# Sparse experts planned twice: 32 tiles of the first ten sequences while the last four are routed, then 40

## The chip, the cores and the metric

One core of one Trainium2 chip runs the whole program. The metric is the device time of one execution in microseconds (us); lower is better. TensorE is called PE in the profile, VectorE DVE, ScalarE ACT, GpSimd POOL and SyncE SP.

## The reference

Two layers over x of 16 sequences x 512 tokens x 128. The first layer (a linear state recurrence and a one-of-eight linear expert) and the second layer's linear attention are the same in both kernels. What the change touches is the second layer's mixture of experts:

```python
def _moe(t, gate_w, gate_b, mlp1_w, mlp1_b, mlp2_w, mlp2_b):   # t: 8192 x 128
    logits = t @ gate_w + gate_b                               # 8 experts
    top_v, top_i = jax.lax.top_k(logits, K)                    # K = 2
    probs = jax.nn.softmax(top_v, axis=-1)
    w = zeros.at[arange(T)[:, None], top_i].set(probs)
    def body(acc, ew):
        h = _swiglu(t @ w1 + b1)     # 128 -> 512 -> 256, min(glu, 7), clip(lin, -7, 7)
        y = h @ w2 + b2              # 256 -> 128
        return (acc + we[:, None] * y, None)
...
ms = jnp.mean(x * x, axis=-1, keepdims=True)
t = (x * jax.lax.rsqrt(ms + EPS) * norm_scale)
return x + y
```

## The kernel before

The program has phases one behind the other; the last one holds the second layer. All engines have their own in-order program in it (`@block.tensor`, `@block.vector` and so on), written out by hand, and they wait for one another through counting semaphores: `need(engine, name, count)`.

*Attention and routing.* A pass n of each engine's loop works on several sequences at once, at different stages: a sequence w is projected in pass w, weighted in w + 1 and routed up to pass w + 8. Routing one sequence of 512 tokens (four slices of 128) is a chain across engines: moments (DVE), 1/sqrt by Ln and Exp (ACT), `normed` (ACT, L1661), `modulated` (DVE), `squares` and a second 1/sqrt (ACT), `payload` (ACT, L1545), `turn_pay` (PE, L2298) and `turned_pay` (ACT), `logits` (PE, L2364), `logits_kept` (ACT), `logits_back` (PE, L2376), `largest` and `chosen` (DVE), `ranks` (PE), `placed` (DVE, position `posu`), and at last eight `send`s: POOL scatters 128 payload rows each by indirect DMA into `rows_of` in DRAM (L1479), where every expert has a region of its own. The POOL's other work in this part is `products` (L1470).

*The plan.* After the last sequence PE adds up how many rows each expert has (L2404), DVE turns this into 72 tiles of 256 rows (L2024 to L2060: the expert and first row of each tile, `meta` and `packs`), SP and ACT write padding rows behind each region, and SP waits for all scatters.

*The tile loop.* 72 tiles v run through the engines. SP loads the 256 rows (`xt`, L1432). PE transposes them (`turn`, L2417), ACT copies the result to SBUF (`turned`, L1725) and copies the expert's first weights and biases out of all experts' into one of two buffers (`own_weights`, L1732). PE makes four matmuls of 128x256 (L2432). DVE adds the bias and clips, glu (L2104) and lin (L2109), ACT takes the gelu of glu (L1747), DVE multiplies (`product`, L2095). Two tiles behind, PE makes the second product (L2446, L2451), ACT scales it by the token's weight (`yw`, L1756; eight buffers), and POOL places both halves, 128 rows each, by indirect DMA into `parts` (L1504). Every fourth tile DVE computes weights and destination rows of four tiles (`weights_and_places`, L2075 to L2088).

*The tail.* When all rows are placed, SP loads `parts` sequence by sequence (L1445), DVE adds the pairs, gates them and adds them to x, and ACT's queue writes the output.

## Time and profile before

| | us |
|---|---|
| median of 3 runs | 1067.23 |
| lowest, highest | 1066.64, 1077.73 |
| span of the profiled execution, first to last instruction | 1003.5 |
| PE busy in the span | 837.3 (83%) |
| DVE busy | 827.6 (82%) |
| ACT busy | 619.4 (62%) |
| POOL busy | 563.5 (56%) |
| DMA traffic | 84.47 MB, mean 84 GB/s |

The profile is of one execution, and its own time is known by its span alone: the first row is time measured from outside, which holds what lies around the span as well. Busy shares are means over phases with different limits; rows from single stretches say more. Idle time of an engine is put down to what ended it; "issue" means that the engine waited for nothing that the profile shows. The clock column is PE's granted clock as a share of 2.4 GHz, 0.50 is 1.2 GHz.

### The profile page before, as it was taken

The page shows a single profiled execution, that of the slowest core. Times are in us where ns is not written, and L with a number is a line of the kernel's source. Part 1 is how long each engine was busy: PE and PEld are TensorE (multiplying, and loading weights), DVE is VectorE, ACT ScalarE, POOL GpSimd, SP SyncE. Part 2 cuts the span into 40 slices and gives each one's busy share as a digit, 9 for nine tenths or more (in the row PEclk, how much of TensorE's full clock was granted, in tenths as well). Part 3 has the DMA queues.
Part 4 walks back from the last instruction along what each step waited for, and adds up shares of the span by engine and source line. Part 5 has one row for each costly group of instructions (what it writes and reads, how often), then busy time and mean ns, then how long its engine had stood idle before and what let it go on. Part 6 is the DMA issues. An engine that isn't in the chain of part 4 may idle for free.

```text
span 1003.5 us, 22806 instructions
## 1 busy us (share of the span) xinstructions
PE 837.3 (83%) x7439; PEld 645.8 (64%) x7439; DVE 827.6 (82%) x2204; ACT 619.4 (62%) x1669; POOL 563.5 (56%) x573
## 2 busy tenths in 40 slices
PE   6887972899999579999999999994149999999900
PEld 6854652444454268888888888883038888889800
DVE  3987769899997586789999999997638888888848
ACT  3475128899983474587787767746236666666600
POOL 1221018568760534336888888887727676767720
PEclk9999895799999879999999999996569999999955
DMA  5230541333233050000111111111243333233168
GB/s 153 82 90 1 143 134 46 130 105 138 90 127 127 9 145 19 2 10 26 37 44 34 37 36 45 36 37 47 95 122 94 89 90 89 89 95 97 54 227 296
DMA packets 74479, 84.47 MB, mean 84 GB/s; under 512 B 14254, under 2 KB 64361, under 8 KB 72188
## 3 DMA queue, kind: packets, MB, share of 16 engines
q1 hardware_dynamic: 56492, 60.06, 19.7%
q0 software_dynamic: 8704, 18.11, 5.4%
q10 hardware_dynamic: 9168, 4.87, 1.6%
q8 instruction: 61, 1.00, 0.4%
q14 instruction: 54, 0.44, 0.2%
HBM read 59.33 MB, written 23.67 MB: 83 GB/s over the span
## 4 chain that ended last, share of the span: by engine, by line
PE 51%; DVE 6%; DMA 2%; issue 2%; POOL 1%; SPq 1%; ACT 1%; POOLq 0%; DVEq 0%; ACTq 0%
PE ps L2432 13%; PE ps L2194 11%; PE ps L2451 6%; PE ps L2210 3%; PE ps L2272 2%; PE ps L2185 2%; PE ps L2417 2%; PE ps L2331 2%; PE ps L2311 2%; PE ps L2205 1%; POOL rows_of L1479 1%; PE ps L2156 1%; PE ps L2171 1%; PE ps L2259 1%; DVE x_tok L2128 1%
## 5 line engine op out<-in xcount | busy, mean ns | idle before, releaser
L1470 POOL TENSOR_TENSOR kvb<-qk,v 128x1024 f32<-128x1024 f32 x64 | 126.7, 1984 | 74.7 <-DVE qk L1854 50.4
L1479 POOL DMA_INDIRECT rows_of<-payb,posu x128 | 144.1, 1126 | 40.6 <-issue 27.0
L1115 PE MATMUL ps<-masked,ew 128*128 128x512 f32 x256 | 129.9, 623 | 4.2 <-DVE masked L1043 3.5
L2194 PE MATMUL ps<-con,kvb 128*128 128x128 f32 x1024 | 126.0, 276 | 0.0
L2194 PEld LDWEIGHTS ps<-con,kvb 128*128 128x128 f32 x1024 | 119.4, 192 | 1.0 <-issue 1.0
L1504 POOL DMA_INDIRECT parts<-h,dest x72 | 72.8, 1011 | 55.0 <-ACT h L1756 33.3
L1043 DVE TENSOR_TENSOR masked<-f_t,wide 128x512 f32<-128x512 f32 x128 | 88.6, 710 | 9.7 <-PE ps L1115 9.4
L1830 DVE TENSOR_TENSOR qc<-ps,qk 128x1024 f32<-128x1024 f32 x64 | 78.0, 1219 | 17.9 <-PE ps L2194 17.3
L1747 ACT ACTIVATE nrm<-qk 128x512 f32<-128x512 f32 x72 | 45.4, 630 | 72.8 <-DVE qk L2104 72.7
L1504 POOL DMA_INDIRECT parts<-gx,dest x72 | 74.9, 1040 | 25.6 <-issue 23.3
L2451 PE MATMUL ps<-w,f_t 128*128 x576 | 76.1, 275 | 0.0
L2451 PEld LDWEIGHTS ps<-w,f_t 128*128 128x128 f32 x576 | 70.0, 192 | 8.3
L1115 PEld LDWEIGHTS ps<-masked,ew 128*128 128x128 f32 x256 | 43.3, 194 | 47.2 <-issue 23.9
L2432 PE MATMUL ps<-qd,ex 128*128 128x256 f32 x288 | 69.3, 384 | 0.7 <-issue 0.7
L2432 PE MATMUL ps<-qd,lg 128*128 128x256 f32 x288 | 68.3, 380 | 0.3 <-issue 0.3
L2432 PEld LDWEIGHTS ps<-qd,ex 128*128 128x128 f32 x288 | 52.8, 193 | 6.8 <-ACT qd L1725 0.9
L2432 PEld LDWEIGHTS ps<-qd,lg 128*128 128x128 f32 x288 | 51.9, 190 | 6.2 <-issue 0.5
L891 ACT ACTIVATE junk<-x_tok,stat 128x128 f32<-128x128 f32 x128 | 49.4, 387 | 10.4 <-DVE stat L1019 9.8
L2095 DVE SCALAR_TENSOR_TENSOR f_t<-qk,nrm 128x512 f32<-128x512 f32 x72 | 50.5, 701 | 6.4
L2104 DVE TENSOR_SCALAR qk<-ps,ex 128x256 f32<-128x256 f32 x72 | 31.5, 478 | 29.3 <-PE ps L2432 29.3
L2417 PE MATMUL ps<-con,kvb 128*128 128x128 f32 x144 | 28.1, 277 | 25.1 <-DMA kvb<-rows_of 25.1
L2104 DVE TENSOR_SCALAR qk<-ps,lg 128x256 f32<-128x256 f32 x72 | 31.5, 478 | 8.1 <-PE ps L2432 8.0
(354 smaller groups left out, 2237.7 us busy)
## 6 DMA issues: line engine op xcount, KB each, us to landing
wide<-hot_dram SPq DMA_DIRECT2D x16, 1024.0 KB, 4.6
kvb<-rows_of SPq DMA_DIRECT2D x72, 132.0 KB, 2.1
toep<-taps_dram SPq DMA_DIRECT2D x16, 512.0 KB, 6.1
x_tok<-in_x_dram SPq DMA_DIRECT2D x16, 256.0 KB, 3.1
out_dram<-x_tok ACTq DMA_DIRECT2D x16, 256.0 KB, 5.6
rows<-rows_dram SPq DMA_DIRECT2D x16, 192.0 KB, 3.2
kvb<-parts SPq DMA_DIRECT2D x6, 512.0 KB, 6.9
rows<-rows_dram SPq DMA_DIRECT2D x16, 128.0 KB, 4.5
```

The lines of the kernel that those rows point to most:

```text
L891: last = nc.scalar.activation(junk[j][:, c, :], source(t), ACT.Square, bias=total[:, t:t + 1], scale=float(D), accum_out=out_sq[:, t:t + 1])
L1043: nc.vector.tensor_tensor(masked[e % 4][:, :], f_t[w % W][:, :], wide[w % W][:, e, :], ALU.mult).then_inc(s["masked"], 1)
L1115: nc.tensor.matmul(ps[:, w % 2, :], ew0[:, e, :], masked[e % 4][:, :], start=False, stop=(e == E - 1)).then_inc(s["product"], 1)
L1470: nc.gpsimd.tensor_tensor(kv[g % KB][:, :, :].rearrange("p e (h d) -> p e h d", h=H), k_in, v_in, ALU.mult).then_inc(s["kv"], 1)
L1479: nc.gpsimd.indirect_dma_start(rows_of, bass.IndirectOffsetOnAxis(ap=posu[w % 2][:, slot, t:t + 1], axis=0), pay[w % PB][:, t, :], None).t ...
L1504: nc.gpsimd.indirect_dma_start(parts, bass.IndirectOffsetOnAxis(ap=dest[:, u, c:c + 1], axis=0), yw[u][:, c, :], None).then_inc(s_out[u], 16)
L1830: nc.vector.tensor_tensor(qc[g % 2][:, :, :], cum(g), q_in, ALU.mult).then_inc(s["qc"], 1)
L2095: nc.vector.scalar_tensor_tensor(act_t[v % 2][:, :, :], lin[v % 2][:, :, :], -6.0, gs[v % 2][:, :, :], ALU.max, ALU.mult).then_inc(m["a"], 1)
L2104: last = nc.vector.tensor_scalar(glu[v % 2][:, f, :], ps[:, bank, f * SP:(f + 1) * SP], w1c[v % 2][:, I2 + f:I2 + f + 1], 7.0, ALU.add, AL ...
L2194: last = nc.tensor.matmul(cum(g)[:, e, :], kv[g % KB][:, e, :], k("upto"), start=True, stop=True)
L2432: last = nc.tensor.matmul(ps[:, bank + f // 2, (f % 2) * SP:(f % 2 + 1) * SP], w1c[v % 2][:, f * P:(f + 1) * P], x_t[v % 2][:, :], start=T ...
L2451: last = nc.tensor.matmul(to, act_t[v % 2][:, j, c * P:(c + 1) * P], w2[:, bass.ds(e * (2 * D) + j * D, D)], start=False, stop=(c == S - 1 ...
```

## The change

The plan is made twice. The first one counts the rows of the first ten sequences (AW = 10), which is enough for 32 full tiles (FT = 32); it stands in DVE's last pass (n = 16) of the attention loop. The tile loop begins right behind the attention. The first 20 tiles form four rounds of five, and the routing of the last four sequences is spread over them: each engine has a `drain(v)` that does one step of the chain after a given tile. The second plan, of 40 tiles for the rest, stands behind tiles 18 to 20 on DVE; SP writes the padding before tile 28 and waits for all scatters before tile 32.

To make room the rest is rearranged. The first weights of a tile come by DMA from DRAM, 256 KB, into four buffers (WC = 4), so ACT's `own_weights` and the scaling of all weights go, and the norm scale is applied in `turned`. glu is made by ACT in two Relu of 128x256 out of PSUM instead of by DVE. The transposed rows and the result have one PSUM bank each instead of two. Results have 16 SBUF buffers (YW = 16). In the tile loop the 1/sqrt of the last sequences are powers on POOL and the two-way softmax is a tanh, all in one ACT table with the gelu.

```diff
+        room = xg[:, :, :].rearrange("p d t -> p (d t)")
         V = 8
         GT = 4
+        AW = 10
+        FT = 32
+        YW = 16
+        assert 2 * C * P * AW - E * (SP - 1) > (FT - 1) * SP
         BT = -(-(2 * TILES // S + E - 1) // V) * V
         NP = BT // V
         parts = nc.dram_tensor("parts", [(2 * TILES + S * BT) * P, D], F32).ap()
...
+            def h_of(w):
+                return h4[w % 2] if w < B - 2 else late_h[w % 2]
...
-            w1c = [q[:, :, :].rearrange("p j t -> p (j t)")[:, 0:WB] for q in (ex, lg)]
+            WC = 4
+            w1c = [(ex, lg)[j // 2][:, j % 2, :] for j in range(WC)]
-            yw = [(h4 + gx)[v // 2][:, S * (v % 2):S * (v % 2 + 1), :] for v in range(V)]
+            yw = [room[:, XT + v * S * D:XT + (v + 1) * S * D].rearrange("p (c d) -> p c d", c=S) for v in range(YW)]
...
+
+                    def pads():
+                        sp.wait_ge(s["place"], 2)
+                        sp.wait_ge(s["padrow"], 2)
+                        for e in range(E):
+                            row = sp.value_load(counts[0:1, e:e + 1], min_val=e * CAP, max_val=(e + 1) * CAP - SP)
+                            sp.dma_start(rows_of[bass.ds(row, SP), :].rearrange("(p c) d -> p c d", c=S), far[:, :, :]).then_inc(s["pads"], 16)
+
+                    def second_part():
+                        sp.wait_ge(s["pads"], 16 * E)
+                        for j in range(PB):
+                            sp.wait_ge(s_scat[j], 16 * SCATTERS * (B // PB))
+                        sp.wait_ge(s["place"], 3)
+                        need(sp, "pay_ps", B)
+
+                    for v in range(BT):
+                        if v == FT - PADS:
+                            pads()
+                        if v == FT:
+                            second_part()
+                        if v % V == 0:
+                            packed = pack_of(sp, v)
+                        at = sp.value_load(meta[0:1, v:v + 1], min_val=0, max_val=E * CAP - SP)
+                        done(sp, "x_ps", v - V)
+                        grouped(sp, "dest", v - V)
+                        sp.dma_start(xt[:, v % V, :, :], rows_of[bass.ds(at, SP), :].rearrange("(p c) d -> p c d", c=S)).then_inc(s_in[v % V], 16)
+                        e = expert_of(sp, packed, v)
+                        done(sp, "h_ps", v - WC)
+                        sp.dma_start(w1c[v % WC], a["w1"][:, bass.ds(e, 1), :].rearrange("p e i -> p (e i)")).then_inc(s_w1[v % WC], 16)
+                        if v == FT:
...
+                    for j in range(WC):
+                        sp.wait_ge(s_w1[j], 16 * (BT // WC))
+                    for v in range(BT - YW, BT):
+                        rows_out(sp, v)
...
+                    def place_rows(v):
+                        done(pool, "yw", v)
+                        for c in range(S):
+                            nc.gpsimd.indirect_dma_start(parts, bass.IndirectOffsetOnAxis(ap=dest[:, v % YW, c:c + 1], axis=0),
+                                                         yw[v % YW][:, c, :], None).then_inc(s_out[v % YW], 16)
+
+                    placed_rows = 0
+                    for v in range(ROUNDS * ROUND):
+                        r, at = divmod(v, ROUND)
+                        if at == 0:
+                            variance_root(B - 2 + r)
+                        if at == 1:
+                            square_root(B - 3 + r)
+                        if at == 4:
+                            for i in range(SCATTERS if r == ROUNDS - 1 else SCATTERS // 2):
+                                send(B - 4 + r, i)
+                        if at == 0 and r:
+                            for i in range(SCATTERS // 2, SCATTERS):
+                                send(B - 5 + r, i)
+                        if v >= 3 and v % 2:
+                            place_rows(placed_rows)
+                            placed_rows += 1
+                    for v in range(placed_rows, BT):
+                        place_rows(v)
...
+                    nc.scalar.preload_act_table_set("gelu_apprx_sigmoid_and_others")
+                    projected(B - 1)
...
-                    def own_weights(t, packed, v):
-                        if t.exists(v):
-                            e = t.expert(packed, v % V)
-                            t.done("h_ps", v - 2)
-                            t.done("lin", v - 2)
-                            nc.scalar.activation(w1c[v % 2][:, :], w1b1[:, bass.ds(e * WB, WB)], ACT.Copy).then_inc(m["w1c"], 1)
...
+                    def drain(v):
+                        r, at = divmod(v, ROUND)
+                        if r >= ROUNDS:
+                            return
+                        if at == 0:
+                            logits_kept(B - 4 + r)
+                            squares(B - 3 + r)
+                        if at == 2:
+                            normed(B - 2 + r)
+                            weigh_late(B - 4 + r)
+                            payload(B - 3 + r)
+                        if at == 3:
+                            turned_pay(B - 3 + r)
+
+                    def turned(v):
+                        if v < BT:
+                            done(act, "h_ps", v - 2)
+                            done(act, "x_ps", v)
+                            nc.scalar.activation(x_t[v % 2][:, :], ps[:, X_PS, 0:SP], ACT.Copy, scale=ns[:, :]).then_inc(m["x_t"], 1)
...
+                        turned(v + 1)
+                        if v < BT:
+                            e = expert_of(act, packed, v)
+                            bank = H_PS + 2 * (v % 2)
+                            done(act, "hg_ps", v)
+                            if v < 2:
+                                need(act, "red", B * C)
+                            for f in range(2):
+                                last = nc.scalar.activation(glu[v % 2][:, f, :], ps[:, bank, f * SP:(f + 1) * SP], ACT.Relu,
+                                                            bias=b1[:, bass.ds(e * NF + f, 1)], scale=-1.0)
+                            last.then_inc(m["glu"], 1)
+                            done(act, "a", v - 2)
+                            done(act, "glu", v)
+                            nc.scalar.activation(gs[v % 2][:, :, :], glu[v % 2][:, :, :], ACT.Gelu_apprx_sigmoid, bias=limit[:, :], scale=-1.0).then_inc(m["gs"], 1)
+                        drain(v)
+                        if v % V == V - 2 and v + 2 < BT:
+                            act.wait_ge(s["place"], 3 if v + 2 >= FT else 1)
+                            ahead = pack_of(act, v + 2)
+                        if v >= 2:
+                            u = (v - 2) % YW
+                            grouped(act, "dest", v - 2)
+                            rows_out(act, v - 2 - YW)
+                            done(act, "y_ps", v - 2)
+                            for c in range(S):
+                                last = nc.scalar.activation(yw[u][:, c, :], ps[:, Y_PS, c * D:(c + 1) * D], ACT.Copy, scale=own[:, 2, u, c:c + 1])
+                            last.then_inc(m["yw"], 1)
...
                         weighted(n - 1, 2)
+                        if n == B:
+                            rows_of_tiles(False)
                         states(n)
...
+                    done_early()
+
+                    def drain(v):
+                        r, at = divmod(v, ROUND)
+                        if v == 0:
+                            residual(B - 1)
+                        if v == 1:
+                            moments(B - 1)
+                        if r < ROUNDS and at == 1:
+                            shifted(B - 2 + r)
+                            logits(B - 4 + r)
+                            largest(B - 4 + r)
+                            chosen(B - 4 + r)
+                        if r < ROUNDS and at == 3:
+                            placed(B - 4 + r)
+                            modulated(B - 2 + r)
+                        if v == PLAN:
+                            tiles_of_experts(True)
+                        if v == PLAN + 1:
+                            experts_of_tiles(True)
+                        if v == PLAN + 2:
+                            rows_of_tiles(True)
+                        if v == PLAN + 4:
+                            added(B - 4)
+                        for w in range(B - 3, B):
+                            if v == PLAN + 5 + 2 * (w - B + 3):
+                                gated(w)
+                            if v == PLAN + 6 + 2 * (w - B + 3):
+                                added(w)
...
                         for u in range(v, v + GT):
-                            t.landed(s_in, u)
-                            t.landed(s_out, u - V, S)
+                            rows_in(dve, u)
+                            rows_out(dve, u - YW)
...
+                            ranked(B - 4 + v // ROUND)
+                        product(v)
+                        if v % GT == 0:
+                            weights_and_places(v)
+                        drain(v)
...
+
+                    def turn(v):
+                        if v < BT:
+                            done(pe, "x_t", v - 1)
+                            rows_in(pe, v)
...
-                                t.done("yw", v - 4)
-                                t.done("a", v - 2)
...
+                    def drain(v):
+                        r, at = divmod(v, ROUND)
+                        if r >= ROUNDS:
+                            return
+                        if v == 0:
+                            back(B - 1)
+                        if at == 1:
+                            logits_back(B - 4 + r)
+                        if at == 2:
+                            ranks(B - 4 + r)
+                        if at == 3:
+                            turn_pay(B - 3 + r)
+                        if at == 4:
+                            logits(B - 3 + r)
+
...
+                    for v in range(BT + 2):
+                        turn(v + 1)
+                        if v < BT:
+                            bank = H_PS + 2 * (v % 2)
+                            done(pe, "x_t", v)
+                            pe.wait_ge(s_w1[v % WC], 16 * (v // WC + 1))
+                            done(pe, "lin", v - 2)
+                            done(pe, "glu", v - 2)
+                            for f in range(NF):
+                                last = nc.tensor.matmul(ps[:, bank + f // 2, (f % 2) * SP:(f % 2 + 1) * SP], w1c[v % WC][:, f * P:(f + 1) * P], x_t[v % 2][:, :],
+                                                        start=True, stop=True)
+                                if f == 1:
+                                    last.then_inc(m["hg_ps"], 1)
+                            last.then_inc(m["h_ps"], 1)
+                        drain(v)
...
+                            done(pe, "yw", v - 3)
+                            done(pe, "a", v - 2)
...
```

POOL, from the scatters of the last sequences to the first tiles, before: eight scatters a sequence (rows_of), then only placings (parts, two a tile).

```order
L1479 DMA rows_of<-payb,posu_217 67584x132 x8
L1479 DMA rows_of<-payb,posu_218 67584x132 x8
L1479 DMA rows_of<-payb,posu_217 67584x132 x8
L1479 DMA rows_of<-payb,posu_218 67584x132 x8
L1504 DMA parts<-h_194,dest 34816x128 x4
L1504 DMA parts<-h_195,dest 34816x128 x4
L1504 DMA parts<-gx_196,dest 34816x128 x4
```

POOL in the changed kernel, from the same place on: the first round and the start of the second.

```order
L1513 TENSOR_SCALAR rv_167<-mv_163 128x4
L1515 TENSOR_TENSOR rv_167<-rv_167,con 128x4
L1521 TENSOR_SCALAR rm_173<-ms_166 128x4
L1523 TENSOR_TENSOR rm_173<-rm_173,con 128x4
L1528 DMA parts<-xg,dest 34816x128 x2
L1487 DMA rows_of<-payb,posu_219 67584x132 x4
L1513 TENSOR_SCALAR rv_168<-mv_164 128x4
L1515 TENSOR_TENSOR rv_168<-rv_168,con 128x4
L1487 DMA rows_of<-payb,posu_219 67584x132 x4
L1528 DMA parts<-xg,dest 34816x128 x2
L1521 TENSOR_SCALAR rm_172<-ms_165 128x4
L1523 TENSOR_TENSOR rm_172<-rm_172,con 128x4
```

Placings now stand between the scatters of a sequence, and the powers (L1515, L1523) behind and ahead of both.

PE around the end of the routing and tile 0, before (L2364 and L2376 are logits, L2417 a tile's transposes, L2432 its first product).

```order
L2298 MATMUL ps<-con,payb 128x128 x4
L2364 MATMUL ps<-p_t,gw 32x128 x4
L2376 MATMUL ps<-con,lg_t 128x128
L2348 MATMUL ps<-taken_206,earlier 128x32
L2349 MATMUL ps<-upto_now_210,one 128x32
L2404 MATMUL ps<-upto_now_210,one 128x8
L2417 MATMUL ps<-con,kvb 128x128 x4
L2432 MATMUL ps<-qd,ex 128x256 x4
```

PE in the changed kernel at tile 3 of the first round (L2539 transposes, L2568 first product, L2423 `turn_pay` of a sequence, L2583 and L2588 second product of tile 1).

```order
L2539 MATMUL ps<-con,xg 128x128 x2
L2568 MATMUL ps<-qd,lg 128x256 x4
L2423 MATMUL ps<-con,payb 128x128 x4
L2583 REGISTER_ALU x2
L2583 ISA
L2583 MATMUL ps<-b2x,one 128x256
L2588 ISA
L2588 MATMUL ps<-w_222,f_t_177 128x128
L2588 ISA
```

A step of the routing now stands between the two products, and the second product is queued behind it.

## Rows read from the trace of the kernel before

**Rows 1.** the stretches of the last third, core 0, columns in the first row

```profile
core 0: us, PE busy (x) PEld busy (x) DVE busy (x) ACT busy (x) POOL busy (x), PEclk, DMA share, GB/s
676.00:686.00 10.00, 6.74 (x79) 5.44 (x78) 8.56 (x26) 6.04 (x23) 7.61 (x8) 0.94 0.18 55
686.00:740.00 54.00, 10.93 (x57) 5.24 (x55) 28.02 (x146) 16.58 (x67) 36.26 (x36) 0.50 0.22 71
740.00:955.00 215.00, 213.31 (x1357) 190.83 (x1357) 185.54 (x504) 140.88 (x358) 141.73 (x138) 0.99 0.32 92
955.00:964.00 9.00, 1.28 (x9) 1.06 (x9) 0.09 (x1) 0.91 (x4) 5.93 (x7) 0.66 0.16 51
964.00:1003.50 39.50, 0.00 (x0) 0.00 (x0) 31.85 (x48) 0.00 (x0) 0.00 (x0) 0.50 0.90 319
```

**Rows 2.** the chain that ended last, 752 to 762 us: start, us, what

```profile
756.17 1.73 PE ps L2432 x8
...
759.12 1.73 PE ps L2432 x8
```

**Rows 3.** timeline of PE at the seam: start, us, instruction, idle before

```profile
685.09 2.07 PE L2272 MATMUL ps<-g_t,wo 128*128 128x512 f32 x2 [2.57 <-DVE g_t L1821]
...
739.31 0.66 PE L2417 MATMUL ps<-con,kvb 128*128 128x128 f32 x2 [24.83 <-DMA kvb<-rows_of]
```

**Rows 4.** groups of POOL, 690:735 and 740:955 us: busy us, mean ns

```profile
L1479 POOL DMA_INDIRECT rows_of<-payb,posu x33 | 33.8, 1024 | 11.7 <-issue 7.6 <-DVE posu L1985 2.6 <-ACT payb L1628 1.2
...
L1504 POOL DMA_INDIRECT parts<-h,dest x72 | 72.8, 1011 | 55.0 <-ACT h L1756 33.3 <-issue 21.4 <-ACT gx L1756 0.3
```

**Rows 5.** timeline of POOL with a backlog

```profile
788.13 0.96 POOL L1504 DMA_INDIRECT parts<-gx,dest  x1 [0.30 <-issue]
789.39 1.39 POOL L1504 DMA_INDIRECT parts<-gx,dest  x1 [0.30 <-issue]
791.08 0.96 POOL L1504 DMA_INDIRECT parts<-gx,dest  x1 [0.30 <-issue]
792.35 1.38 POOL L1504 DMA_INDIRECT parts<-gx,dest  x1 [0.30 <-issue]
```

**Rows 6.** timeline of all engines, end of the tile loop

```profile
961.85 0.96 POOL L1504 DMA_INDIRECT parts<-gx,dest  x1 [0.30 <-DMA parts<-gx,dest]
964.17 0.81 SPq L1445 DMA_DIRECT2D qk<-parts  x2
```

**Rows 7.** timeline of DVE, first and last cast of the plan

```profile
716.62 0.16 DVE L2036 CAST cnti<-cnt 128x8 int32<-128x8 f32 x1
...
722.93 0.32 DVE L2060 CAST meta<-row 128x72 int32<-128x72 f32 x1
```

**Rows 8.** timeline of ACT (two rows), and a group of ACT, 740:955 us

```profile
692.52 1.64 ACT L1661 ACTIVATE h<-x_tok,sh,rv 128x128 f32<-128x128 f32 x4
...
697.78 1.26 ACT L1545 ACTIVATE payb<-h,rm 128x128 f32<-128x128 f32 x4
...
L1732 ACT ACTIVATE lg<-xg 128x516 f32 x36 | 23.0, 640 | 0.2 <-issue 0.2
```

**Rows 9.** groups of POOL, 0:500 us: power and small op

```profile
L829 POOL TENSOR_TENSOR rs<-rs,con 128x4 f32<-128x4 f32 x16 | 18.0, 1123 | 1.3
...
L827 POOL TENSOR_SCALAR rs<-stat 128x4 f32<-128x4 f32 x16 | 4.5, 279 | 18.2 <-ACT junk L891 17.6
```

**Rows 10.** timeline of POOL: last scatter of rows, first placing

```profile
733.65 0.95 POOL L1479 DMA_INDIRECT rows_of<-payb,posu  x1 [0.30 <-issue]
752.65 0.95 POOL L1504 DMA_INDIRECT parts<-h,dest  x1 [18.05 <-ACT h L1756]
```

**Rows 11.** timeline of ACT, the table load of the tile loop

```profile
741.94 1.28 ACT L1747 ACT_TABLE_LOAD   x1
```

**Rows 12.** timeline of DVE beside rows 5: the product of lin and gs

```profile
789.25 0.69 DVE L2095 SCALAR_TENSOR_TENSOR f_t<-qk,nrm 128x512 f32<-128x512 f32 x1
...
792.21 0.69 DVE L2095 SCALAR_TENSOR_TENSOR f_t<-qk,nrm 128x512 f32<-128x512 f32 x1
```

502 lines of the change are left out of this document (234 added, 268 removed).

## The prediction

> **What bounds the kernel now.** I read the stretches first, then single timelines at the seam. The changed part is the last third of the span. From 740 us to 955 us TensorE is busy 213 of 215 us at full clock [rows 1]: the tile loop of the sparse experts. Two tiles on, the same eight matmul records of L2432 start 2.95 us later [rows 2], so 72 tiles cost 72 x 2.95 = 212.4 us and nothing but TensorE counts there; VectorE (185.5 us), ScalarE (140.9 us) and GpSimd (141.7 us) have room. Ahead of it lies the hole that the change aims at: the last attention matmul of weight is L2272 at 685.09 us, the first transpose of tile 0 stands at 739.31 us [rows 3], and between 686 and 740 us TensorE is busy 10.9 of 54 us at clock 0.50 [rows 1]. What runs there is the routing of the last sequences, and GpSimd: 33 scatters of routed rows with 1.02 us each in 690 to 735 [rows 4] and 0.30 us between two (789.09 to 789.39 is such a pause [rows 5]). Behind the loop the 39.3 us from 964.17 us (first load of the tail, one landing time of 2.3 us after the last placing at 961.85 [rows 6]) are DMA bound, share 0.90 [rows 1], and are not touched. The end of the kernel is thus the time of that first load plus a constant.
>
> The profiled execution has a span of 1003.5 us; the median of the runs is 1067.2 us, 63.7 us more, which lies around the span. I take that as constant and add differences of the span to the median. A difference under 1% (10.7 us) is about what a measurement cannot tell from none.
>
> **The change, part by part.**
>
> *Start of tile 0.* TensorE has first to end the attention: 685.09 + 2.07 = 687.2 us [rows 3]. The first plan is now written into VectorE's last pass, ahead of the product on which L2272 waits. Before, the plan took from 716.62 to 723.25 us, 6.6 us [rows 7]. Now it treats 32 tiles instead of 72; the four passes over tile x expert shrink from 0.75 us to some 0.4, so about 5.2 us (bounds: 3, if some of it falls into VectorE's idle time, and 6.6). VectorE has little such time (busy 8.6 of 10 us before 686 [rows 1]). Tile 0 starts at 687.2 + 5.2 = 692.4 us, 46.9 us earlier than 739.31. The loads of its rows and weights were issued ahead and lie beside.
>
> *The work of a tile.* TensorE keeps its matmuls: 2.95 us. ScalarE loses the weight copy of 0.64 us [rows 8] and takes two Relu of 128x256 out of PSUM; no such row stands in the loop, a bound from below is nothing, from above the whole 0.64 us copy each. Even 1.28 - 0.64 us more on 140.9 / 72 = 1.96 us stays at 2.6 us, under 2.95. VectorE loses work. The weights by DMA are 256 KB a tile; the 16 DMA engines are at 0.32 in the loop at 92 GB/s [rows 1], and 256 KB each 2.95 us are 89 GB/s more: some 0.3 of share, hidden, since four buffers let them come three tiles ahead. Cost nothing; without that cover each tile would wait for a landing, 2.3 us for a placing [rows 6]. The single banks for transposed rows and results add waits on ScalarE's answers that come over a microsecond early.
>
> *The routing moved between tiles.* On TensorE it was 10.9 us at half clock, so 5.5 us at full [rows 1]. On ScalarE it was 16.6 us for four sequences: per round of five tiles 4 us beside 5 x 2. On GpSimd it is heavy, and this is where I look. GpSimd's program after the last product is: 32 scatters of four sequences, 5 pairs of small op and power, and 144 placings. A placing takes 1.01 us in the mean [rows 4] plus the 0.30 pause and some second spent waiting: I use 1.33 us as the mean (0.96 + 0.30 = 1.26 undisturbed [rows 5]). A round then asks 8 x 1.33 + 4.5 placings x 1.33 + a power pair of 1.9 us (1.12 + 0.28 [rows 9] and pauses) = 18.5 us of GpSimd; TensorE wants 5 x 2.95 + 1.4 = 16.1 us. GpSimd is longest.
>
> *GpSimd's sum.* In the kernel before, the first placing started 13.3 us after tile 0 (752.65 [rows 10] against 739.31). Now the table load of 1.28 us [rows 11] is out of this, but the squares, normed rows (1.64 us [rows 8]), payload (1.26 us [rows 8]) and labels of the first round are in front of the first result on ScalarE: + 5 us. First placing at 692.4 + 13.3 - 1.3 + 5 = about 709 us. Until then GpSimd idles. From there to the last scatter of the last sequence it has 32 + 16 DMAs and 3 power pairs: 48 x 1.33 + 3 x 1.9 = 69.5 us, so S = 778.5 us. After it stand 128 placings in a row. TensorE, at tile 24, meets VectorE's destination group, which needs tile 11 placed and landed (16 result buffers): 8 DMAs and a landing, S + 13.4; then 48 x 2.95 + 5 = 147 us, so TensorE ends at about S + 160.
>
> *The price of a placing when GpSimd has a backlog.* The rows show it: 0.96, 1.39, 0.96, 1.38 us [rows 5]. The long ones start 0.14 us into VectorE's L2095 (789.25, 792.21 us), the product of lin and gs [rows 12]. A scatter that starts inside it is held for 0.43 us. And it is a trap: 2 x 1.26 + 0.43 = 2.95 us, the period of the tile, so the next one starts 0.14 us into the next product again. In the kernel before the trap breaks every fourth tile, when the destination group pushes VectorE (busy 86%), and the mean stays 1.33. The changed kernel takes two ops of 128x256 a tile from VectorE, its product comes regularly, and I expect the trap to hold longer. Bounds per DMA while TensorE runs: 1.26 and 1.475 us. I take 1.40, between the mean of the rows and the trap. In S + 0 to S + 160 this is 114 placings; 14 are left at 1.26 us = 17.3. The last starts at S + 176, its landing and the first tail load at 956.8 us, against 964.17: 7.4 us earlier. **Forecast 1067.2 - 7.4 = 1059.8, say 1060 us.** With 1.33 for all 128: S + 170.3, load at 949.8, 1052.8 us. With 1.475: 19.5 placings are left, 24.6 us, load at 964.1, 1067.1 us.
>
> The Trainium skill, page "SBUF — State Buffer", section "Who interferes with whom", says that a VectorE instruction with two SBUF inputs contends with a GpSimd instruction that reads SBUF, and that the one issued first holds the port for its whole length. By that rule each placing caught would be held until the product ends; the trace agrees with the direction (1.39 against 0.96 us [rows 5]). The rule by itself gives the 1067.1 us above.
>
> **The rivals.**
>
> *GpSimd undisturbed.* Scatters and placings run at 1.26 us as most rows do: 709 + 176 x 1.26 + 5.7 = 936.5, load at 937.5, 26.7 us earlier: 1040.5 us. This is a floor as long as GpSimd orders the end; anything from there to the mean of the rows, 1041 to 1053 us, belongs here. For it: in most of the loop the durations are 0.96. Against: [rows 5], and that those short ones partly come from waiting out of phase.
>
> *TensorE bound, as planned.* If GpSimd kept up, the whole distance from tile 0 to the tail stays as it was, 964.17 - 739.31 = 224.9 us, plus 5.5 us of routing: 692.4 + 230.4 = 922.8, 41.4 us earlier, 1025.8 us. Against: GpSimd alone has 176 x 1.26 us after its first placing.
>
> *The rounds come late (slower).* In three rounds TensorE's turn of the payload waits for ScalarE's payload, and that for a power on GpSimd that stands behind four scatters and up to two placings (10 us) in order. TensorE then idles and cools: 2.57 us idle before L2272 and it runs at 1.2 GHz, 2.07 us [rows 3]; a tile in that state is nearly twice as long. Five such waits of 3 us with their cold tiles make the rounds some 15 us longer; S is 793 and, with the trap, the load comes at 979.1 us: 14.9 us later, 1082 us. It decides slower by over 1% from S = 789 us on. For it: each of TensorE, ScalarE and GpSimd has 16 to 18.5 us a round and each waits for the others in order. Against: the chain has one tile of slack at each step.
>
> **How the numbers follow.** Forecast case (GpSimd orders the end at 1.33 to 1.475 us, 1053 to 1067 us) 0.42; undisturbed GpSimd 0.26; TensorE bound 0.07; late rounds 0.25. The range reaches from 1041, the floor of the undisturbed case, to 1083, the late rounds: left out are the TensorE case and the rounds still later, under 0.2 together. Faster by over 1% means under 1056.5: 0.26 + 0.07 + 0.07 of the forecast case = 0.40. Slower by over 1%: 0.20 of the late rounds. Within 1%: 0.40.
>
> **What would show it.** Right: GpSimd without idle time from the first placing to the end, 12 or more tiles behind ScalarE at the end of TensorE, and 20 us or more between TensorE's last matmul and the tail's first load (now 7); placings of 0.96 and 1.39 us in turn. Start of tile 0 near 692, last scatter of routed rows near 778 us. Wrong: if placings wait for results in the second half (then TensorE or ScalarE orders the end and a tile's period tells which); if tile 0 starts after 700; if the tile period is over 3 us (ScalarE, weights or rows late); if a gap stands at tile 32, where the second plan, eight pad writes and all scatters are waited for. I expect none there, as tile 32 comes 35 us after the last routed row.

## The result: 1090 us beside 1070, slower by 1.9%

| | before | after |
|---|---|---|
| median (lowest to highest), us | 1070.5 (1066.6 to 1077.7), 4 runs | 1090.3 (1089.0 to 1092.4), 4 runs |
| ratio, 95% interval | | 1.0186 (1.013 to 1.0242) |
| profiled execution: span | 1003.5 | 1087.2 (its own time 1088.96) |

I had forecast 1060 us within 1041 to 1083. The last row of the table is the first thing to see: after's span is 1.8 us under its own time, while I had put 63.7 us around the span of before. Of the page of the kernel after:

```profile
span 1087.2 us, 23320 instructions
PE 868.7 (80%) x7425; PEld 665.0 (61%) x7440; DVE 774.8 (71%) x2083; ACT 650.8 (60%) x1731; POOL 563.9 (52%) x583
...
PE   6887935999995799999999999578663588888820
...
POOL 1310047478714343388888888426627545555520
PEclk9898965999998799999999999689876689999955
...
PE 35%; ACT 8%; another core or an unknown queue 7%; DVE 7%; issue 7%; SPq 2%; POOL 1%; DMA 1%; ACTq 1%; DVEq 0%; POOLq 0%
```

TensorE has holes in the last third, and 7% of the chain is put down to "another core", though there is only one. In the rows below the same stands as "remote": a wait for which the profile finds no releaser. The stretches of after, cut at tile 0, tile 24 and the last tile (columns: us; busy us and count of each engine; granted clock, DMA share, GB/s), answer to [rows 1]:

```profile
686.00:705.30 19.30, 9.73 (x73) 7.47 (x73) 10.35 (x38) 5.27 (x12) 9.26 (x10) 0.59 0.42 119
705.30:857.50 152.20, 90.45 (x476) 74.51 (x475) 62.55 (x250) 72.66 (x204) 77.64 (x80) 0.79 0.30 90
857.50:1028.00 170.50, 148.91 (x895) 127.61 (x895) 87.76 (x242) 114.68 (x282) 92.00 (x95) 0.97 0.52 156
1028.00:1087.20 59.20, 10.58 (x55) 8.74 (x53) 36.48 (x57) 6.55 (x18) 10.21 (x11) 0.58 0.64 225
```

Tile 0 is early as meant (705.3 against 739.3 us [rows 3]), but the first 24 tiles take 152 us with TensorE busy 90 of them, and the other 47 take 170 us where 47 x 2.95 would be 139. GpSimd does not order the second part: its groups behind 690 us (busy us, mean ns; idle before, by releaser) answer to [rows 4]:

```profile
L1528 POOL DMA_INDIRECT parts<-xg,dest x144 | 141.3, 981 | 111.6 <-ACT xg L1816 80.0 <-issue 31.6
L1487 POOL DMA_INDIRECT rows_of<-payb,posu x40 | 41.4, 1035 | 50.4 <-issue 26.9 <-DVE posu L2048 23.6
```

80 us of the placings' idle time are waits for ScalarE's results. A tile that nothing disturbs still takes 2.95 us: two transposes of L2539, and the matmuls of L2568 behind them, in after's timeline of TensorE:

```profile
813.04 0.38 PE L2539 MATMUL ps<-con,xg 128*128 128x128 f32 x2
813.26 1.89 PE L2568 MATMUL ps<-qd,ex 128*128 128x256 f32 x8
...
815.99 0.38 PE L2539 MATMUL ps<-con,xg 128*128 128x128 f32 x2
816.21 1.89 PE L2568 MATMUL ps<-qd,ex 128*128 128x256 f32 x8
```

**What a hole looks like.** After's timeline of all engines, 783 to 796 us (start, us, instruction, idle before it and releaser):

```profile
783.58 1.15 PE L2588 MATMUL ps<-w,f_t 128*128 x8
...
785.85 0.72 ACT L1805 ACTIVATE nrm<-qk,limit 128x512 f32<-128x512 f32 x1
...
786.79 0.96 POOL L1487 DMA_INDIRECT rows_of<-payb,posu  x1 [0.30 <-issue]
...
794.38 0.96 POOL L1528 DMA_INDIRECT parts<-xg,dest  x1 [0.30 <-issue]
795.39 0.69 DVE L2217 SCALAR_TENSOR_TENSOR f_t<-qk,nrm 128x512 f32<-128x512 f32 x1 [8.12 <-remote]
795.45 0.63 ACT L1816 ACTIVATE xg<-ps,own 128x128 f32<-128x128 f32 x2 [8.72 <-remote]
```

VectorE's product and ScalarE's result wait for one thing in common, the end of TensorE's results of tile 13 (L2588). Those matmuls end at 784.73 us. The trace also keeps the times at which each semaphore was raised, and this one was raised at 795.37 us, 10.6 us late, as GpSimd's row of DMAs ended (794.38 + 0.96 = 795.34). The longest hole stands behind a row of 30 DMAs with 0.30 us between them:

```profile
849.89 0.96 POOL L1528 DMA_INDIRECT parts<-xg,dest  x1 [0.30 <-issue]
854.46 0.69 DVE L2217 SCALAR_TENSOR_TENSOR f_t<-qk,nrm 128x512 f32<-128x512 f32 x1 [17.10 <-remote]
854.55 0.63 ACT L1816 ACTIVATE xg<-ps,own 128x128 f32<-128x128 f32 x2 [23.50 <-remote]
855.45 0.96 POOL L1528 DMA_INDIRECT parts<-xg,dest  x1 [4.59 <-ACT xg L1816]
...
855.51 0.39 PE L2583 MATMUL ps<-b2x,one 128*128 x1 [25.83 <-ACT xg L1816]
```

TensorE's signal from 826.00 us was raised at 854.44. ScalarE's result (L1816) waited for it, and TensorE in turn stood 25.8 us ahead of L2583, since the one result bank was not emptied. Tile 24 starts 31.7 us behind tile 23.

The Trainium skill ("Perfetto Trace Analysis", section "Tensor Engine Instruction (MATMUL, LD_WEIGHTS)") says that a matmul's reported end is an estimate and that the semaphore is pushed only once PSUM has acknowledged the writes, outside the profiled window. The rows above agree that such time is not in TensorE's own records: it shows only as idle time of those who wait.

### The profile page after: what moved, and what is told of

Same layout as the page of the kernel before. It is cut to its first block, busy times and chain, and to the rows that moved or that the text cites. A ratio compares the mean times of both kernels' runs of the same rounds, so it can differ in the third digit from the quotient of the medians.

```text
span 1087.2 us, 23320 instructions
## 1 busy us (share of the span) xinstructions
PE 868.7 (80%) x7425; PEld 665.0 (61%) x7440; DVE 774.8 (71%) x2083; ACT 650.8 (60%) x1731; POOL 563.9 (52%) x583
## 4 chain that ended last, share of the span: by engine, by line
PE 35%; ACT 8%; another core or an unknown queue 7%; DVE 7%; issue 7%; SPq 2%; POOL 1%; DMA 1%; ACTq 1%; DVEq 0%; POOLq 0%
PE ps L2319 10%; PE ps L2568 4%; PE ps L2335 3%; ACT qk L1800 2%; PE ps L2588 2%; ACT nrm L1805 2%; ACT xg L1816 2%; PE ps L2384 2%; PE ps L2310 2%; PE ps L2397 1%; PE ps L2281 1%; PE ps L2330 1%; PE ps L2436 1%; ACT qd L1785 1%
## 5 line engine op out<-in xcount | busy, mean ns | idle before, releaser
L1528 POOL DMA_INDIRECT parts<-xg,dest x144 | 141.3, 981 | 111.6 <-ACT xg L1816 80.0
L2229 DVE TENSOR_SCALAR qk<-ps,b 128x256 f32<-128x256 f32 x144 | 62.9, 478 | 106.8 <-remote 69.9
L2319 PE MATMUL ps<-con,kvb 128*128 128x128 f32 x1024 | 127.7, 278 | 0.0
L1800 ACT ACTIVATE qk<-ps,b 128x256 f32<-128x256 f32 x144 | 60.6, 476 | 50.2 <-PE ps L2568 24.1
L1816 ACT ACTIVATE xg<-ps,own 128x128 f32<-128x128 f32 x144 | 44.6, 359 | 73.2 <-remote 56.1
L2588 PE MATMUL ps<-w,f_t 128*128 x576 | 86.9, 299 | 0.0
L2588 PEld LDWEIGHTS ps<-w,f_t 128*128 128x128 f32 x576 | 77.0, 208 | 5.4 <-issue 0.6
L2568 PE MATMUL ps<-qd,lg 128*128 128x256 f32 x288 | 74.8, 407 | 0.0
L2568 PE MATMUL ps<-qd,ex 128*128 128x256 f32 x288 | 72.5, 397 | 0.0
L2583 PE MATMUL ps<-b2x,one 128*128 x72 | 20.9, 290 | 64.1 <-ACT xg L1816 57.4
L2568 PEld LDWEIGHTS ps<-qd,lg 128*128 128x128 f32 x288 | 56.8, 208 | 7.3
L2568 PEld LDWEIGHTS ps<-qd,ex 128*128 128x128 f32 x288 | 55.2, 202 | 6.7
L1805 ACT ACTIVATE nrm<-qk,limit 128x512 f32<-128x512 f32 x72 | 52.0, 722 | 6.9
```

The costliest lines, as they stand in the source:

```text
L1528: nc.gpsimd.indirect_dma_start(parts, bass.IndirectOffsetOnAxis(ap=dest[:, v % YW, c:c + 1], axis=0), yw[v % YW][:, c, :], None).then_inc( ...
L1800: last = nc.scalar.activation(glu[v % 2][:, f, :], ps[:, bank, f * SP:(f + 1) * SP], ACT.Relu, bias=b1[:, bass.ds(e * NF + f, 1)], scale=-1.0)
L1805: nc.scalar.activation(gs[v % 2][:, :, :], glu[v % 2][:, :, :], ACT.Gelu_apprx_sigmoid, bias=limit[:, :], scale=-1.0).then_inc(m["gs"], 1)
L1816: last = nc.scalar.activation(yw[u][:, c, :], ps[:, Y_PS, c * D:(c + 1) * D], ACT.Copy, scale=own[:, 2, u, c:c + 1])
L2319: last = nc.tensor.matmul(cum(g)[:, e, :], kv[g % KB][:, e, :], k("upto"), start=True, stop=True)
L2568: last = nc.tensor.matmul(ps[:, bank + f // 2, (f % 2) * SP:(f % 2 + 1) * SP], w1c[v % WC][:, f * P:(f + 1) * P], x_t[v % 2][:, :], start= ...
```

## The experiments

I paired each instruction behind 690 us that raises a semaphore with the raise that the trace recorded before the next one on the same semaphore. "Late" is over 0.3 us. Some records are missing, and a signal raised only after the next one's end gets no partner or a wrong one, so the column shows how common late signals are and no more. For each kernel's profiled execution: span, start of tile 0, tiles 0 to 24, tiles 24 to 71 (starts), and late signals of TensorE of those paired. Ratios are to the kernel before on the same chip, with 95% intervals; the traces come from several chips, so differences of a few us between rows say little.

| kernel | ratio | span | tile 0 | 0-24 | 24-71 | late |
|---|---|---|---|---|---|---|
| page of before | | 1003.5 | 739.3 | 69.6 | 138.8 | 0/228 |
| ctl_before | 1.0011 (0.9983-1.0038) | 1056.3 | 754.7 | 79.8 | 162.9 | 80/207 |
| ctl_after | 1.0221 (1.0158-1.0285) | 1081.3 | 703.2 | 152.7 | 167.1 | 135/262 |
| w1_four | 1.0145 (1.0099-1.0192) | 1078.9 | 702.7 | 154.5 | 163.6 | 126/271 |
| y_banks | 1.0185 (1.0138-1.0232) | 1074.5 | 701.3 | 153.4 | 162.7 | 114/270 |
| before_plain | 0.9591 (0.9529-0.9653) | 1015.4 | 755.5 | 70.3 | 138.8 | 2/229 |
| before_half | 0.9583 (0.9525-0.9642) | 1022.0 | 761.5 | 70.4 | 138.6 | 6/188 |
| after_plain | 0.9601 (0.9533-0.9669) | 1011.1 | 701.0 | 112.3 | 145.4 | 21/292 |
| plain_spread | 0.9488 (0.9451-0.9524) | 1007.1 | 703.0 | 102.7 | 148.8 | 3/285 |
| rounds_first | 1.0037 (1.0011-1.0063) | 1060.3 | 744.8 | 90.2 | 166.9 | 163/262 |
| rounds_y | 0.9946 (0.9921-0.9971) | 1052.8 | 744.4 | 87.8 | 163.5 | 135/255 |
| rounds_y_spread | 1.0003 (0.9978-1.0029) | 1066.6 | 754.3 | 86.2 | 167.5 | 125/253 |
| rounds_gap4 | 0.9995 (0.9970-1.0021) | 1070.8 | 749.8 | 90.9 | 173.9 | 163/264 |
| before_gap4 | 1.0118 (1.0044-1.0192) | 1077.4 | 762.1 | 82.3 | 174.1 | 53/201 |
| after_gap4 | 1.0100 (1.0037-1.0164) | 1080.2 | 708.0 | 133.1 | 182.7 | 131/267 |
| after_spread | 1.0071 (1.0049-1.0094) | 1067.5 | 702.1 | 109.6 | 197.0 | 117/247 |
| after_spread_y | 1.0036 (1.0006-1.0066) | 1065.4 | 702.6 | 109.9 | 196.4 | 106/256 |
| two_first_y | 1.0101 (1.0062-1.0140) | 1071.4 | 727.1 | 120.0 | 166.8 | 131/255 |

The same pairing over whole traces tells more of where late signals stand. GpSimd's first indirect DMA starts at 458 to 465 us. Ahead of it not one of TensorE's 440 paired signals is late in any of the 19 traces; behind it 27 to 186 of some 380 to 480 are, in all but the page of before, which has none. ScalarE's signals (159 to 305 a trace behind 690 us) are never late, VectorE's seldom (5 of 315 in ctl_before, by 1.1 us at most). DMA traffic as such does not do it: in ctl_before it is 85 GB/s ahead of 460 us and 81 in the tile loop.

### The kernel before once more

The same code as before, profiled again.

> The kernel before, unchanged, to see its span beside its time. Its profiled span was 1003.5 us while its timed runs took 1066.6 to 1077.7; the kernel after has 1087.2 beside 1088.96. Theory A (before has a fast kind of execution and a usual one 64 us longer, and my sum was made against the rare one): most spans here are about 1065 us, and the tile loop takes more than 72 x 2.95 us. Theory B (64 us lie around the span): span 1003, time 1067.

Median 1060.95 us, span 1056.3 beside its own time of 1059.72. Theory A. The page of my forecast was of an execution 53 us shorter than this one. It must be rare: the spans recorded with some 90 timed runs of before lie between 1053.8 and 1075.6 us, none near 1003.5. Of the 53 us, 15.4 stand ahead of tile 0, 34.3 between tile 0 and tile 71, 3.1 behind. Of the 15.4, some 14 are there before the last attention matmul (L2272), beside the scatters of earlier sequences. The registers that SyncE sets for the row loads tell the two apart at a glance (min/median/max ns). On the page of before:

```profile
L1432 SPq FUSED_REGOPS  x72: 37/42/42, 736.9 to 927.8; - x72
L1432 SPq MOVE kvb<-rows_of x72: 29/29/29, 737.0 to 927.9; - x72
```

and in the control run:

```profile
L1432 SPq FUSED_REGOPS  x72: 3/42/708, 752.3 to 975.5; - x72
L1432 SPq MOVE kvb<-rows_of x72: 3/29/707, 752.4 to 976.0; - x72
```

The control's stretches, which answer to [rows 1]:

```profile
686.00:754.70 68.70, 16.03 (x117) 9.63 (x116) 33.39 (x162) 20.81 (x84) 40.98 (x40) 0.55 0.18 58
754.70:997.30 242.60, 216.90 (x1314) 188.38 (x1315) 177.94 (x487) 139.33 (x345) 135.29 (x132) 0.98 0.28 81
```

Even VectorE's own chain is held beside GpSimd's scatters. The plan took 6.6 us [rows 7] on the page and 14.3 us here (730.57 to 744.90), with rows such as

```profile
742.45 0.23 DVE L2057 SCALAR_TENSOR_TENSOR row<-expert,row 128x72 f32<-128x72 f32 x1 [1.07 <-DVE row L2056]
743.83 0.23 DVE L2058 TENSOR_REDUCE packf<-digits 128x9 f32<-128x72 f32 x1 [1.15 <-DVE row L2057]
```

### The kernel after once more

> The kernel after, unchanged, on this chip and beside the others. 1.0186 times the kernel before, as first measured, so near 1080 us.

1083.65 us, 1.0221. Control against control, after's tile 0 is 51.5 us earlier (754.7 to 703.2), its 71 tile distances take 77.1 us more (242.7 to 319.7), the tail 0.6 less: 25.0 us more. Of the 77, 72.9 fall on tiles 0 to 24.

### Weights for four tiles only

```
-  sp.dma_start(w1c[v % WC], a["w1"][:, bass.ds(e, 1), :]...)
+  if v < WC:
+      sp.dma_start(w1c[v % WC], a["w1"][:, bass.ds(e, 1), :]...)
```

> The kernel after, but only the first four tiles load their weights; the other 68 use what lies in the buffers (leaves out 68 weight loads of 256 KB). Theory 1 (weights by DMA, their traffic or their turn in SyncE's queue, delay the tiles): 1090 falls by 20 us or more, and the pair of tiles behind tile 32 comes down from 7.0 to 5.9 us. Theory 2 (the tiles wait for GpSimd, the single result bank and the rounds): 1088 to 1092, no change.

1076.21 us, where before took 1060.68 on this chip. The ratio's interval (1.0099 to 1.0192) overlaps that of ctl_after (1.0158 to 1.0285); in the traces the span is 2.4 us shorter and tiles 24 to 71 3.5 us. Theory 2, in the main: the weights by DMA cost little, by the two ratios at most some 8 us, though the DMA share behind tile 24 falls from 0.52 to 0.30. Late signals stay as common.

### A second PSUM bank for results

```
+  def y_bank(v): return 7 if v >= FT and v % 2 else Y_PS
-  done(pe, "yw", v - 3)
+  done(pe, "yw", v - 4 if v - 2 > FT else v - 3)
```

> The kernel after, but from tile 33 on the results of odd tiles go to a second PSUM bank, and TensorE waits for the result before last instead of the last. Theory 1 (the 4.05 us of every second tile come from the single result bank): pairs of 5.9 us behind tile 32, 39 tiles x 0.55 = 21 us less, 1069 us, if GpSimd (2.53 us a tile) keeps up. Theory 2 (signals of TensorE reach the others late for another reason): the pair stays near 7.0 us, 1090.

1078.03 us and 1.0185, no change by the ratio; tiles 24 to 71 lose 4.4 us of the 21 expected. The single bank is not what makes the tiles behind tile 33 long; my first theory for it fell. Ahead of tile 33, where the longest hole is, the bank stayed single here, and after with two banks from tile 1 wasn't run.

### No placing by index

```
+  def store(v):      # SyncE
+      done(sp, "yw", v)
+      sp.dma_start(parts[v * SP:(v + 1) * SP, :]..., yw[v % YW]).then_inc(s_out[v % YW], 16)
   def place_rows(v): # GpSimd
+      return
```

> The kernel after, but SyncE stores each tile's results in the order of the tiles with one plain DMA, and GpSimd issues no placing at all (leaves out the placing by index; the 32 scatters of routed rows stay). Theory S (TensorE's signals reach the other engines late while GpSimd issues indirect DMAs, and that holds up the tiles): after the last scatter the tiles run at 2.95 us each without late signals, TensorE's last tile is over 60 us earlier and the time falls to 1010 us or less. Theory R (the order of waits in the new tile body itself, its single banks or its weights by DMA cost 0.6 us a tile): the period behind tile 32 stays near 3.5 us and the time stays above 1060.

> The kernel before with the same edit: plain stores by SyncE in place of the placings by index. Theory S: its 72 tiles take 212 us as on the page of the kernel before, not the 255 us of the control run, and the time falls by 40 to 50 us, to some 1010 to 1020. Theory R, or another cause of the 53 us between page and control: 1055 to 1060.

1016.15 and 1017.21 us: 67.5 us under ctl_after and 41.4 us under the kernel before, all on one chip. Theory S, though after_plain stays 6 us above the 1010 that I had named, and its tiles behind tile 24 take 3.09 us each, not 2.95. Before's loop without placings is the one of its page (209.1 against 208.4 us), and TensorE is busy throughout:

```profile
755.50:964.60 209.10, 207.91 (x1315) 185.53 (x1316) 178.27 (x490) 136.74 (x345) 0.00 (x0) 0.99 0.32 95
```

Late signals fall from 80 to 2 and from 135 to 21. The edit also takes GpSimd's own work off the tiles, so by itself it does not separate late signals from placings that GpSimd gets to late. For before the page does: there GpSimd makes all its placings, no signal is late, and the loop takes 208.4 us. Without placings the change neither wins nor loses.

### One placing a tile, with a rest

Before with plain stores, and besides one placing a tile into a tensor that nobody reads.

> The kernel before with plain stores of all results by SyncE, and besides one placing by index a tile by GpSimd (the first 128 rows, into a tensor that nobody reads), so that GpSimd has 1.7 us of rest between two. Theory S1 (a signal of TensorE waits only while GpSimd's indirect DMAs follow each other without a longer rest): nearly the time without placings, 1017 to 1025. Theory S2 (each indirect DMA costs the tiles its share, 41 us for 144): halfway, 1038 us.

1023.66 us; the ratio is that without placings (0.9583 and 0.9591).

```profile
761.50:970.50 209.00, 207.71 (x1314) 185.51 (x1315) 178.29 (x490) 136.66 (x345) 63.99 (x67) 0.99 0.39 115
```

GpSimd is busy 64 us in it and TensorE loses nothing: 72 indirect DMAs with a rest behind each are free, where 144 cost 41 us. That fits theory S1, that their following each other is what costs. A kernel with all 144 and a rest behind each wasn't run.

### A rest behind every fourth tile's placings

```
   place_rows(v):
+      if v % 4 == 3:
+          nc.gpsimd.tensor_tensor(pause[...], k("ones")[:, 0:4], k("minus_half")[:, 0:4], ALU.pow)
```

> The kernel after, with one more GpSimd operation of 1.04 us behind the placings of every fourth tile, so a rest of 1.6 us in each row of eight placings. Theory S1: held signals get through in the rest, the 31 us hole shrinks to 12 or less; 10 to 25 us less than the kernel after, 1060 to 1073 us. Theory S2, or GpSimd as bound: no gain, 1084 to 1095.

> The same extra operation in the kernel before. Theory S1: its loop (243 us for 72 tiles on the control run) falls towards 209, a gain of 5 to 25 us, 1035 to 1053. Theory S2: GpSimd gets 18 x 1.3 us more to do, same or slower: 1058 to 1070.

> All routing ahead of tile 0 as in the run with the rounds first, and the extra operation of every fourth tile. Theory S1: the loop of 257 us falls by 10 to 30, 1033 to 1053 us. Theory S2: 1063 or more.

None of the three came out wholly as theory S1 had it. After comes nearest: the ratio falls from 1.0221 to 1.0100, some 13 us, though the intervals overlap by a hair (the one begins at 1.0158, the other ends at 1.0164). The longest hole falls from 31.6 to 21.5 us, not to 12 (tiles 0 to 24: 152.7 to 133.1), and tiles 24 to 71 rise by 15.6 us. Before gets 1.2% slower (24 to 71: 162.9 to 174.1) although fewer of its signals are late (53 of 201). With the rounds first no change can be told: 0.9970 to 1.0021 beside 1.0011 to 1.0063 without the rests. My reading, which no run shows by itself: a rest of 1.6 us per eight placings is too rare to free the signals and makes GpSimd late itself, since its 2.53 us a tile leave it 0.42.

### Rounds ahead of tile 0

Every engine does its part of all rounds, and the second plan, before tile 0.

> The kernel after, but each engine does all of its part of the four rounds of routing and the second plan before tile 0, with no placing in between; the tile body, the weights by DMA and the ring of 16 results stay. Theory S and the rounds (mixing GpSimd's scatters with tiles makes each signal of TensorE late in a chain that needs it): tile 0 starts 50 us or more later, but the tiles then run without the 31 us hole, and the whole is 0 to 20 us faster than the kernel after. Theory R (the tile body costs): the loop is as slow as before and the whole is 30 us or more slower than the kernel after.

1063.09 us, 1.0037: theory S and the rounds, with tile 0 41.6 us later than in ctl_after, not 50 or more, and the first 24 tiles 62.5 us shorter. The new tile body is not free, though: its loop takes 257.1 us against 242.7 in ctl_before, 14.4 us more, and tile 0, 9.9 us earlier, hides most of it.

### Rests between the scatters

```
   send(B - 4 + r, i)
+  if i % 2:
+      rest()      # the power of 1.04 us, into a column of its own
```

> The kernel after with plain stores by SyncE (no placing by index, as in the run of 1016 us), and a GpSimd operation of 1.04 us behind every second of the 32 last scatters of routed rows, so that TensorE's signals have a rest. Theory S (late signals make the rounds slow): tiles 0 to 24 take 112 us without the rests and fall to 95 or less, the time to about 1000 us. Theory C (the chain of the rounds through four engines is slow by itself): 110 to 120 us for the 24 tiles, the time 1015 to 1025.

> The kernel after itself (with its placings) and the same rests between the 32 last scatters. Theory S: rests free the signals in the rounds but make GpSimd later by 16 x 1.3 = 21 us, so its row of placings behind the last scatter stays or grows: 1070 to 1090 us. Theory C: 1090 to 1105.

Without placings the rests take the late signals from 21 to 3 and tiles 0 to 24 from 112.3 to 102.7 us; the time falls to 1007.92. The ratio, 0.9488 (0.9451 to 0.9524), now lies 1% under that of before without placings (0.9529 to 0.9653). Both theories have a part: 9.6 us go, 102.7 stay where undisturbed tiles need 70. What stays is the chain and the rounds' own work. The waits of after_plain, 700 to 820 us (total us, times, longest us), show the chain: the scatters wait for positions, and TensorE waits for VectorE's prefix sums.

```profile
POOL rows_of L1495 <- DVE posu L2053: 51.1, 4, 15.5
...
PE ps L2478 <- DVE upto_now L2020: 15.9, 3, 7.6
```

With placings, the rests bring 43 us in tiles 0 to 24 (109.6), and 30 of them come back behind tile 24 (197.0), where ScalarE now stands 26 us once: GpSimd's row of placings behind the last scatter is 32 long. The net is 1.0071 where after has 1.0221.

### In search of a better version

> All routing ahead of tile 0, and two PSUM banks for the results from tile 1 on. With a second bank TensorE can go on while a signal is held. Theory S: the loop of 257 us falls by 5 to 15 us, so 1045 to 1058 beside 1063 with one bank: at or under the kernel before. Otherwise no change from the run with the rounds first (1.004 times before).

> Two of the four rounds ahead of tile 0, two between the tiles, and two result banks from tile 33 on. Theory S: fewer scatters between tiles, a shorter row of placings behind the last scatter and a shorter hole than 31 us; between the kernel after (1.02 times before) and the run with all rounds first (1.004), 1.00 to 1.01 times before. If the loss came from the rounds' position and not from GpSimd's rows: 1.02 as the kernel after.

> All routing first, two result banks, and the rests between the last 32 scatters. Theory S: signals of the routing ahead of tile 0 come sooner, but GpSimd is what the routing there waits for; tile 0 within 5 us of 744, time 1050 to 1058. A gain of more than 5 us over the run without rests would mean that the signals, not GpSimd, order the routing.

> The kernel after with the rests between its last 32 scatters and two result banks from tile 33 on: both gains together, 1060 to 1068 us, still not under the kernel before, since the row of some 30 placings behind the last scatter stays.

rounds_y, with all routing first and a second result bank from tile 1 on, is the one version under the kernel before: 1055.15 us, 0.9946 (0.9921 to 0.9971). Of 0.9% against rounds_first the spans show 7.5 us, 5.8 of them in the loop. It was picked as the best of 11 complete versions, and half a per cent is little. Half the rounds first comes to 1.0101 (1.0062 to 1.0140), between all rounds first and none, as expected, and is no better than none with rests. The rests with all rounds first were a miss: tile 0 at 754.3 instead of 744.4, outside my 5 us, and 1.0003. Where GpSimd orders the routing they are lost time. after_spread_y comes to 1.0036 and is not under before, as expected.

## Why the prediction was wrong

**The step that failed** is "The profiled execution has a span of 1003.5 us; the median of the runs is 1067.2 us, 63.7 us more, which lies around the span. I take that as constant and add differences of the span to the median". Only 1.7 to 3.4 us lie around a span (ctl_before: 1059.72 against 1056.3). The rest was inside the timed executions and not in the profiled one, and with it came late signals of TensorE, which stand beside GpSimd's rows of indirect DMAs. The 63.7 us themselves drop out of a difference; what does not is that I priced every wait from rows where no such thing happens (0 late signals of 228), and reasoned about GpSimd only as a queue with a length, not as a thing that goes with others being slowed.

The term of the sum that came out wrong is the distance from tile 0 to the tail's first load. I had it grow by 39.5 us (224.9 to 264.4); control against control it grew by 76.7 (262.2 to 338.9). Within it I had tile 24 start at S + 13.4 = 791.9, 99.5 us behind tile 0; it was 152.7 us. The start of tile 0 came 51.5 us earlier where I had 46.9, and the tail behind its first load stayed as it was, as I had it (39.4 and 39.2 us).

Point by point:

- *Tile period 2.95 us, weights by DMA at nothing:* held where nothing is late; w1_four puts the DMA at 2 to 4 us in the traces. "A gap at tile 32": none, as said.
- *Tile 0 at 692.4 us:* 705.3. The term of 5.2 us for the plan held in kind, but a signal of TensorE (L2492, 694.54 us) was raised 8.2 us late, at 702.74, and VectorE stood 6.8 us before L1880 began at 702.67.
- *First placing at 709, last scatter S = 778.5:* 722.8, and 822.7 us. This is past the 789 us from which I had the change slower by over 1%. So of my cases the late rounds come nearest, with 1082 us, but in part by luck. The wait that I had named, TensorE's turn of the payload for ScalarE's payload, costs 2.8 us in all in after's first 24 tiles. TensorE stands 35.1 us for ScalarE's results and 10.0 for VectorE's prefix sums. Of the 82.7 us that ctl_after's first 24 tiles take over 70, some 32 are the rounds themselves (plain_spread), 10 go with signals late beside scatters, and 40 go when the placings do (after_plain against ctl_after). Not all of the 40 is shown to be late signals: the one hole of 31.6 us behind a signal held 28.7 us is most of it, but without placings GpSimd also reaches its scatters and powers sooner. Some 7 of the 40 are TensorE's own work at a lower clock (busy 90.4 us at a granted 0.78 against 83.2 at 0.88). I had given the case five waits of 3 us.
- *"After it stand 128 placings in a row", GpSimd orders the end:* the row was there for 22 DMAs from 822.7 us. Then TensorE, whose next tile came 31.7 us behind the last, had nothing more to hand over, and GpSimd idled 80 us for ScalarE from the first placing to the last. Its last placing starts 2.3 us behind TensorE's last result (1045.4 and 1043.1 us), where I had 16. The sign that I had named for being wrong, "if placings wait for results in the second half", is what stands there.
- *The trap at 1.40 us a placing:* the mean was 0.981 us plus 0.30. The Trainium skill's rule ("SBUF — State Buffer", section "Who interferes with whom") gave the forecast case its upper end; in after's rows the longest of 144 placings is 1.459 us and most have 0.96, so the contention is seen but not the lock-step.
- *TensorE bound, 1025.8 us:* without placings the kernel gives 1016 us, but so does before. The early start of 54.5 us (755.5 to 701.0) is spent by 48.5 us in the loop, 42 of them in tiles 0 to 24. Even with all placings gone the change wins nothing that can be measured; it takes the rests between the scatters as well to win 1% (plain_spread), and before was not run with such rests.

So where did the expected gain go? 51.5 us were won at the start and 77.1 lost again in the loop: the routing between tiles makes a chain of single handovers among four engines, where each of TensorE's can be late beside a row of GpSimd's DMAs, and it leaves the placings of the first tiles as one long row behind the last scatter.

**What stays open.** Why an execution can have no late signals at all, with the same rows of 32 scatters at 0.30 us (the page of before), and on what the others depend. Whether placings that GpSimd reaches late cost anything beside the late signals in after (a rest behind each of its 144 placings would tell). Whether recording has a part in the late signals: each timed run comes with a span of its own, so no time without any recording is at hand. Whether the delay is of the matmuls' writes or of the signal: a kernel that tells these apart wasn't tried. The parts of 32, 10 and 40 us are differences of single traces on two chips.

## What to carry to other kernels

Compare the span with the profiled execution's own time and with the timed runs before adding anything up: the 60 us "around the span" meant here that the page was of another kind of execution, and a second profile of the unchanged kernel is the cheapest run there is. Where GpSimd issues indirect DMAs back to back, reckon with late signals of TensorE, and look for waits put down to "remote" or "another core" in a kernel of one core. Here, routing in one block and a second result bank did better (0.9946) than a chain interleaved with the tiles (1.0221); rests between the scatters helped that chain (1.0071) and cost time where GpSimd was what the others waited for (1.0003 instead of 0.9946).

## What was not expected of the hardware

- A signal of TensorE can be raised 28.4 us after its matmul's recorded end (826.00 to 854.44 us) while GpSimd issues a row of 0.96 us DMAs with 0.30 us between them. One such DMA every 2.95 us holds nothing up (209.0 us for 71 tile distances, as without).
- Held signals come in order, and some close together: those of 784.73, 784.95, 785.81, 786.68 and 787.11 us were raised at 795.37, 797.50, 797.56, 797.62 and 797.65 us. Within the row of 30 (812.60 to 850.86 us) a few get through, each later than the one before: in order of the raises, those of 816.15, 817.24 and 818.10 us at 822.74, 829.14 and 836.18 us.
- It is nearly only TensorE's signals that are late: 135 of 262 in ctl_after, where none of ScalarE's some 200 and VectorE's some 230 is. In no trace is one of them late ahead of GpSimd's first indirect DMA (0 of 440).
- SyncE's register moves, 29 ns each when undisturbed, take up to 707 ns in the control run's tile loop (three of 72 over 0.5 us), and at 851 to 854 us, beside a row of GpSimd's DMAs, three of SyncE's steps take 681 to 707 ns each.
